# The first expert layer of a decoder on the 14 picked tokens of each batch alone

## The reference, cut to what matters

```python
B, T, C = x.shape                      # 16, 56, 128
cap = int(2.0 * T / 8)                 # 14 tokens for each of 8 experts, in each batch
probs = softmax(einsum('BTC,CE->BTE', x, gate_w), axis=-1)
top_p, top_idx = top_k(transpose(probs, (0, 2, 1)), cap)
xin = take_along_axis(x[:, None, :, :], top_idx[..., None], axis=2)
h = gelu(einsum('BElC,ECH->BElH', xin, w1), approximate=False)     # H = 512
y = einsum('BElH,EHC->BElC', h, w2) * top_p[..., None]
out = zeros((B, T, C)).at[b_idx, top_idx].add(y)
```

## Time and profile before

| | |
|---|---|
| median of 3 runs | 1523.01 us (1521.43 to 1523.82) |
| the profiled execution: its time | 1522.98 us |
| its span, first to last instruction | 1521.2 us |
| PE busy in the span | 1426.3 us (94%) |
| DVE busy | 1087.2 us (71%) |
| ACT busy | 898.9 us (59%) |
| POOL busy | 804.3 us (53%) |
| granted TensorE clock, mean | 0.973 of 2.4 GHz |

### The profile page before, as it was taken

One profiled execution on the slowest core, in us unless ns is written; L12 is line 12 of the kernel. 1 busy time (PEld: TensorE's weight loads), 2 busy tenths in 40 slices (PEclk: granted clock), 3 DMA queues, 4 the chain that ended last, 5 costly groups with the idle time before them and its releaser, 6 DMA issues.

```text
span 1521.2 us, 25506 instructions
## 1 busy us (share of the span) xinstructions
PE 1426.3 (94%) x9258; PEld 1057.2 (69%) x9258; DVE 1087.2 (71%) x2089; ACT 898.9 (59%) x1879; POOL 804.3 (53%) x440
## 2 busy tenths in 40 slices
PE   7889999999999999999999977799999999997898
PEld 4547888888888888888668644455556555553587
DVE  5538887888878888888269674677777777780587
ACT  3427666666667766666257533366666666654475
POOL 4136444444444444431046182198888888898363
PEclk9999999999999999999999998899999999997899
DMA  3032222222222222210223120454635445220221
GB/s 80 27 110 54 53 54 54 53 54 54 54 54 54 54 53 54 54 32 15 87 66 114 42 63 21 112 133 97 147 84 133 112 105 140 62 62 1 81 85 56
DMA packets 72363, 107.23 MB, mean 70 GB/s; under 512 B 14430, under 2 KB 54694, under 8 KB 72110
## 3 DMA queue, kind: packets, MB, share of 16 engines
q1 hardware_dynamic: 59326, 90.53, 24.0%
q10 hardware_dynamic: 12912, 15.08, 3.3%
HBM read 66.52 MB, written 2.08 MB: 45 GB/s over the span
## 4 chain that ended last, share of the span: by engine, by line
PE 84%; DVE 8%; issue 2%; ACT 2%; POOL 2%; DMA 1%; SPq 1%; ACTq 0%; POOLq 0%; DVEq 0%
PE PS L637 9%; PE PS L1014 7%; PE PS L651 6%; PE PS L625 5%; PE PS L1028 5%; PE PS L994 5%; PE PS L626 5%; PE PS L627 5%; PE PS L653 5%; PE PS L652 5%; PE PS L1331 4%; PE PS L1333 3%; PE PS L1332 3%; PE PS L959 3%; PE PS L965 3%
## 5 line engine op out<-in xcount | busy, mean ns | idle before, releaser
L1117 POOL TENSOR_TENSOR QO_area<-QO_area,prob_a 125x896 f32<-125x896 f32 x160 | 336.0, 2100 | 27.8 <-ACT prob_a L1202 6.4
L796 ACT ACTIVATE HL<-PS 125x512 fp32r<-125x512 f32 (+1 forms) x384 | 206.6, 539 | 178.6 <-PE PS L637 159.4
L880 DVE TENSOR_TENSOR HL<-PS,HL 125x512 fp32r<-125x512 f32 (+1 forms) x384 | 237.8, 622 | 75.9 <-ACT HL L796 56.1
L1266 DVE TENSOR_REDUCE QO_area<-PS 112x1 f32<-112x500 f32 x384 | 238.6, 670 | 66.3 <-PE PS L994 66.3
L1202 ACT ACTIVATE prob_a<-PS 125x448 f32<-125x448 f32 x384 | 187.6, 540 | 108.4 <-PE PS L1014 105.4
L710 POOL TENSOR_TENSOR HL<-ctx_area,ones 125x512 fp32r<-125x512 f32 (+1 forms) x64 | 93.1, 1454 | 247.1 <-PE PS L653 195.5
L651 PE MATMUL PS<-HL 125*128 125x512 f32 (+1 forms) x384 | 155.6, 405 | 3.6 <-DVE HL L880 3.3
L625 PE MATMUL PS<-HL 128*128 128x500 f32 x336 | 152.9, 455 | 5.6 <-POOL HL L713 5.6
L1014 PEld LDWEIGHTS PS<-HL 98*125 98x125 f32 x768 | 103.9, 188 | 72.0 <-ACT prob_a L1202 38.2
L806 ACT ACTIVATE prob_a<-prob_a,neg_max 128x500 f32<-128x500 f32 x192 | 135.5, 706 | 29.7 <-DVE neg_max L872 28.4
L994 PE MATMUL PS<-HL 96*112 96x500 f32 x384 | 129.6, 414 | 22.9 <-DVE QO_area L1266 12.3
(11 more groups left out here) (200 smaller groups left out, 2995.1 us busy)
## 6 DMA issues: line engine op xcount, KB each, us to landing
HL<-prob_b SPq DMA_DIRECT2D x128, 187.5 KB, 4.0
ctx_area<-in_ctx_T SPq DMA_DIRECT2D x16, 750.0 KB, 13.1
ctx_area<-in_ctx SPq DMA_DIRECT2D x16, 750.0 KB
HL<-ctx_area SPq DMA_DIRECT2D x64, 187.5 KB, 3.8
QO_area<-gates_kept ACTq DMA_DIRECT2D x16, 448.0 KB, 3.7
inv_area<-in_ctx_T SPq DMA_DIRECT2D x8, 750.0 KB, 4.5
prob_a<-in_ctx_T SPq DMA_DIRECT2D x8, 750.0 KB, 4.3
inv_area<-inv_kept ACTq DMA_DIRECT2D x16, 256.0 KB, 3.4
```

The costliest lines, as they stand in the source:

```text
L880: nc.vector.tensor_tensor(pL[k % 3][0:KC, 0:width(g)], PS[0:KC, 2 + k % 3, 0:width(g)], pH[k % 3][0:KC, 0:width(g)].bitcast(fp32), ALU.sub ...
L1117: nc.gpsimd.tensor_tensor(late_acc[b % 2], before, late_p[n % LATE_P], ALU.add).then_inc(m["padd"], 1)
L1266: nc.vector.tensor_reduce(late_part[b % 2][:, u // NKB, u % NKB:u % NKB + 1], PS[0:2 * S, u % NKB, 0:KB], AX, ALU.max).then_inc(m["mx"], 1)
```

## The change

The first expert layer gets functions of its own (sparse_*), and the second keeps the old ones. In the new ones every expert sees only its picked tokens, 224 columns (256 in the products, since the operands reach into what lies beside).

- **Gather.** PE turns XN into rows of tokens for each batch. DVE makes the mask of picks, PE turns it and multiplies it with a triangular matrix of ones (a running count, so each picked token gets a slot from 1 to 14), and DVE compares the slots with 1 to 14 to get a one-hot matrix of 56 x 112 (8 experts x 14 slots) for each batch. Sixteen fp32 products of token rows with one-hot matrices give the picked columns, split by ACT and DVE into xg_hl.
- **Experts.** Each has 12 matmuls for the hidden tiles and 12 for the output, of 256 columns; one gelu, one high and one low part over 4 x 224 = 896 elements, and a copy of 224 output columns. Order on PE: hidden product of expert e + 2, then output product of expert e.
- **Put back.** 16 transposes of the outputs, copies, and 16 products with `scatter` (112 x 896: the gate where the row's slot is the token's, else 0) give the sum over experts; DVE adds it to X once. `scatter` is made from the gates and the slots, which go to DRAM and come back by 16 loads of 14 partitions each, all on SP's queue.
- **Weights.** Four buffers for each weight in place of two (WBUF), and POOL starts to split when the last scores of the cross-attention are done. SP loads experts 0 and 1 before it takes back vo_kept, experts 2 and 3 after the last softmax transposes, 4 to 7 as buffers come free.
- **Constants** (a ramp of 1 to 14, the triangular matrix) are made on DVE behind the cross-attention.

The diff, cut to its core:

```diff
+            for b in range(B):
+                mm = nc.tensor.transpose(PS[0:S, b // 4, (b % 4) * 128:(b % 4 + 1) * 128],
+                                         XN[:, b * S:(b + 1) * S], ident[:, :])
...
+            hold_clock(2)
+            pe.wait_ge(m["gates"], 1)
+            nc.tensor.transpose(PS[:, 5, 0:S], routed, ident[0:S, 0:S]).then_inc(m["gtr"], 1)
+            hold_clock(3)
+            pe.wait_ge(m["picked"], 1)
+            nc.tensor.transpose(PS[0:S, 4, 64:192], work[:, 0:S], ident[:, :]).then_inc(m["slots"], 1)
+            pe.wait_ge(m["mtc"], 1)
+            nc.tensor.matmul(PS[0:S, 4, 192:320], tri[1], mask_T, start=True, stop=True).then_inc(m["slots"], 1)
+            hold_clock(1)
+            for i in range(4):
+                pe.wait_ge(m["bankc"], i + 1)
+                pe.wait_ge(m["hot"], i + 1)
+                for j in range(4):
+                    b = 4 * i + j
+                    mm = nc.tensor.matmul(PS[:, i, j * SLOTS:(j + 1) * SLOTS], tok_rows[:, b, :],
+                                          onehot[:, b, :, :].rearrange("p e r -> p (e r)"), start=True, stop=True)
+                mm.then_inc(m["bank"], 1)
...
+            def hidden_product(e):
+                pe.wait_ge(m["w1sp"], e + 1)
+                if e == 0:
+                    pe.wait_ge(m["bankc"], 8)
+                    pe.wait_ge(m["xlo"], 4)
+                if e >= 2:
+                    pe.wait_ge(m["hact"], e - 1)
+                first, off = picked_at(e)
+                for f in range(NF):
+                    mm = three_passes(PS[:, 2 * (e % 2) + f // 2, (f % 2) * 256:(f % 2 + 1) * 256],
+                                      [w[:, f * 128:(f + 1) * 128] for w in sw1_hl[e % WBUF]],
+                                      [x[:, first:first + 256] for x in xg_hl], True, True)
+                mm.then_inc(m["h"], 1)
...
+            hidden_product(0)
+            hidden_product(1)
+            for e in range(E):
+                if e + 2 < E:
+                    hidden_product(e + 2)
+                output_product(e)
...
+            pool.wait_ge(xa0["scores"], UNITS * B)
+            for e in range(E):
+                i = e % WBUF
+                pool.wait_ge(ld_sw[i], 32 * (e // WBUF + 1))
+                if e >= WBUF:
+                    pool.wait_ge(m["h"], e - WBUF + 1)
+                halve(sw1_hl[i], sw1[i], m["w1sp"])
+                if e >= WBUF:
+                    pool.wait_ge(m["y"], e - WBUF + 1)
+                halve(sw2_hl[i], sw2[i].rearrange("p g d -> p (g d)"), m["w2sp"])
...
+            sp.wait_ge(m["kept"], 32)
+            for dst, kept in ((gate_re, gates_kept[0]), (slot_re, slot_kept)):
+                for e in range(E):
+                    sp.dma_start(dst[e * CAP:(e + 1) * CAP, :],
+                                 kept[e * B:(e + 1) * B, :].rearrange("(a b) s -> a (b s)", a=1)
+                                 .broadcast_to([CAP, NTOK])).then_inc(ld_re, 16)
...
+            low(0)
+            low(1)
+            for e in range(E):
+                keep_output(e)
+                if e + 2 < E:
+                    low(e + 2)
+                if e == 2:
+                    dve.wait_ge(ld_re, 16 * 2 * E)
+                    nc.vector.scalar_tensor_tensor(scatter, slot_re, slot_col, gate_re, ALU.is_equal, ALU.mult)\
+                        .then_inc(m["scat"], 1)
...
             cross_sync(sp)
+            for e in range(2):
+                sparse_weights(sp, e)
             take_fold(sp)
...
-            experts_sync(sp, 0)
+            for e in range(2, E):
+                sparse_weights(sp, e)
+            sparse_sync(sp)
```

More of the change, by code:

```diff
@@ L263, in decoder_kernel @@
         names = "logit gexp gsub gates gtr picked kept rows xsp w1sp w2sp h hact hhi hlo y ymul b2mm".split()
-        ff = [{n: sem(f"ff{l}_{n}") for n in names} for l in range(2)]
-        ld_w = [[sem(f"ld_w{l}{i}") for i in range(2)] for l in range(2)]
-        ld_gates = [[sem(f"ld_gates{l}{i}") for i in range(2)] for l in range(2)]
+        ff = {n: sem(f"ff_{n}") for n in names}
+        ld_w = [sem(f"ld_w{i}") for i in range(2)]
+        ld_gates = [sem(f"ld_gates{i}") for i in range(2)]
+        names = "mtc hot bank bankc xlo slots slc kept wbe scat h hact hhi hlo y yc ytcd out".split()
+        sf = {n: sem(f"sf_{n}") for n in names}
+        for n in "logit gexp gsub gates gtr picked w1sp w2sp".split():
+            sf[n] = ff[n]
+        ld_sw = ld_w + [sem(f"ld_sw{i}") for i in range(2, WBUF)]
+        ld_re = sem("ld_re")
         class Chain:
@@ new lines, in sparse_gpsimd, with halve @@
+        def sparse_gpsimd(pool):
+            m = sf
+            def halve(hl, x, signal):
+                nc.gpsimd.tensor_tensor(hl[0], x, ones[:, 0:1].broadcast_to([128, FF]), ALU.mult)\
+                    .then_inc(pool_step, 1)
+                pool_count[0] = pool_count[0] + 1
+                pool.wait_ge(pool_step, pool_count[0])
+                nc.gpsimd.tensor_tensor(hl[1], x, hl[0].bitcast(fp32), ALU.subtract).then_inc(signal, 1)
+            pool.wait_ge(xa0["scores"], UNITS * B)
[8 more added lines that the diff above has]
+                halve(sw2_hl[i], sw2[i].rearrange("p g d -> p (g d)"), m["w2sp"])
@@ L1329, in experts_tensor @@
+        def experts_tensor(pe, n):
+            m = ff
+            pe.wait_ge(xn_ready, 2 * n + 2)
+            for b in range(B):
+                mm = nc.tensor.matmul(PS[0:S, 6, b * WCOLS:(b + 1) * WCOLS], XN[:, b * S:(b + 1) * S],
+                                      gate_w[1][:, :], start=True, stop=True)
             mm.then_inc(m["logit"], 1)
@@ L1488, in experts_scalar, with experts_vector @@
                         high(e + 1, f - 1)
-            if l == 0:
-                nc.scalar.preload_act_table(ACT.Sqrt)
-        def experts_vector(dve, l, chain):
-            m = ff[l]
-            ng = E if l == 0 else WCOLS
+        def experts_vector(dve, chain):
+            m = ff
             G = gate[:, :, 0:E]
@@ L1505, in experts_vector @@
             st = [gate_stat[:, k, :] for k in range(4)]
[L1506 to L1513 removed]
+            dve.wait_ge(m["logit"], 2)
@@ L1514, in experts_vector @@
+            logits = PS[0:S, 6, 0:B * WCOLS].rearrange("p (b e) -> p b e", b=B)
+            chain.link(dve, nc.vector.tensor_tensor(
+                gate[:, :, :], logits,
+                gate_b[:, :].rearrange("p (a e) -> p a e", a=1).broadcast_to([S, B, WCOLS]), ALU.add))
             chain.link(dve, nc.vector.tensor_reduce(st[0], G, AX, ALU.max))
             nc.vector.tensor_tensor(G, G, per_batch(st[0]), ALU.subtract).then_inc(m["gsub"], 1)
-            dve.wait_ge(m["gexp"], 1)
+            dve.wait_ge(m["gexp"], 2)
@@ new lines, in experts_vector @@
+            chain.link(dve, nc.vector.tensor_reduce(st[1], gate2[:, :, :], AX, ALU.add))
+            chain.link(dve, nc.vector.tensor_scalar(st[2], st[1], 0.0, None, ALU.is_equal))
+            chain.link(dve, nc.vector.tensor_tensor(st[3], st[1], st[2], ALU.add))
+            chain.link(dve, nc.vector.reciprocal(st[0], st[3]))
+            nc.vector.tensor_tensor(by_expert, gate2[:, :, :], per_batch(st[0]), ALU.mult)\
+                .then_inc(m["gates"], 1)
+            dve.wait_ge(m["gtr"], 2)
```

359 lines of the change are left out of this document (260 added, 99 removed).

## The result

| | before | after |
|---|---|---|
| median of 4 runs | 1522.22 us (1520.83 to 1523.82) | 1482.9 us (1482.68 to 1486.01) |
| the profiled execution | 1522.98 us | 1482.68 us |
| ratio | | 0.975, 95% interval 0.9733 to 0.9768 |

A forecast was written before the change was run, and what follows sets the result against it. PE bounds the old stage, POOL the new one. 15.9 + 33.9 + 5.1 = 54.9 us for 88.2, so -33.3, and -1.9 earlier: 1522.98 - 35.2 = 1487.8, about 1488 us; range 1480 to 1500, the forecast's own 1483 to 1493.

The forecast's parts named there:

- POOL takes over: Expert stretch: POOL's weight splits are slowest from expert 4 on, 4.7 to 6.9 us an expert against PE's 2.9.
- a, the front: From the first logits product to the first hidden product: 15.9 us (14.3 to 19), with the gather's clock uncertain.
- b, the experts: From the first hidden product through the expert products: 33.9 us (28.5 to 40), set by POOL's splits slowed by DVE.
- rival 1: Experts: POOL runs free of DVE and the clock stays up; stretch 28.7 us, total 1482 to 1483; chance 0.15.
- c, putting back: Stage's end, output copy, transposes, scatter products and additions to X: 5.1 us (4.5 to 7), against 2.2 before.
- d, the end of the cross-attention: 1 MB of loads out of the inv_kept write's way, so ACT should not wait: -1.9 us (0 to -2.8).
- Costed at nothing: DVE's constants behind the cross-attention's last product (about 5 us uncovered) and the scatter matrix's loads, delay up to 6 us free.
- rivals 4 and 5: Scatter loads late by 8 to 12 us, total 1490 to 1494, chance 0.07; or landing serially, about 1 us slower, chance 0.02.
- one of the three signs that the prediction named for being wrong: Wrong if PE never waits for POOL, stage clock is near 0.5, or next layer's norm starts at another clock level.
- rival 2: Whole stage: the clock stays at 1.2 GHz, a 256-column pass taking 0.213 us; total 1500; chance 0.13.
- rival 3: Experts: a 256-column pass costs what 448 columns cost, 0.20 us; stretch near 41 us, total 1495; chance 0.04.

The follow-up runs named there:

- more_bufs: Against the changed kernel: six split buffers for w1 and five for w2 instead of four each, w1 of the next expert split before w2; 1478.73 us, ratio 0.9719.
- two_pass: The changed kernel without the third pass (low x high) of the new expert products, 128 passes instead of 192; 1482.31 us, ratio 0.9746.
- no_fill: The changed kernel without the six filler products on PE between the logits and the gather; front 18.40 us, 1492.28 us in one run.
- low_memset: The changed kernel with the low part of the hidden values set to zero by DVE instead of computed; 1481.64 us, ratio 0.9741.
- late_loads: The changed kernel with the loads of experts 0 and 1 back behind the projection weights, as before the change; 1488.77 us in one run.
- before_2: The kernel before the change, unchanged, run again for a second trace; 656.3 us behind the stage, against 658.5 in the first.
- after_2: The changed kernel, unchanged, run again for a second trace; experts 33.32 us, 1484.31 us in one run.
- after_3: The changed kernel, unchanged, run again on one chip with a repeat of more_bufs; experts 33.34 us, 1484.76 us, ratio 0.9759.

## Why the prediction was right

**What bounds the kernel, and that POOL takes over** held: PE was idle between products, POOL worked without a pause from 797.06, and more_bufs and two_pass show it from both sides (less waiting for POOL: -6.5; less work for PE: -0.8 to -1.8).

**a, the front: 15.4 for 15.9.** The terms were each right within some tenths. The clock, "the question here", was full through the gather, where I took a value between full and half. The fillers did it, as no_fill shows.

**b, the experts: 32.4 for 33.9**, and three terms moved in it. Output product 0 ended 7.8 behind the first pass (7.3 predicted, with 1.1 in it for a low clock; 16 passes at 0.213 for 0.119 are 1.5, and in the other two traces of after, with about 27 such passes, it ended at 8.7). The six splits took 815.0 - 797.06 = 17.95 where I had 14.1 + 5.2 = 19.3: the loss to DVE is 17.95 - 14.1 = 3.85. Five DVE instructions with two inputs lie in that time (low parts 2 to 5 and `scatter`), so 0.77 for each, as predicted from the earlier trace rows; I had counted six and a half. In low_memset the same six splits took 2.8 us less with four of the five gone, 0.7 for each. By the Trainium skill, "SBUF — State Buffer", section "Who interferes with whom", the port lock would cost POOL the whole of each DVE instruction. The traces agree on who disturbs whom (the memsets of low_memset, with no input, cost POOL nothing). On the amount the trace of after does not: DVE's low part itself took 1.62 beside POOL for 1.09 alone, and POOL lost less than that. The one `scatter` of low_memset came nearer to it: there POOL lost 0.96 (2.00 for 1.04) and `scatter` took 1.03. Last, the 48 passes behind w1 of expert 7 took 6.6 for 5.8 + 1.5: the clock did fall in a gap that POOL left, but the slow passes were hidden. The low bound of this term was summed wrongly: 33.9 less 5.2 for contention and 1.1 and 1.5 for the clock is 26.1, not 28.5, so rival 1, with a clock that stays up, would have begun near 1480 and not at 1482.

**c, putting back: 6.7 for 5.1**, near the top of its range of 4.5 to 7. The term that was mis-sized is "the last four products (0.5)": the products fill two halves of X one after another, 16 instructions each, so all 3.74 us of L1444 stand in the path, and 1.85 lie between the two additions. From the end of the last copy (824.15 + 0.69 = 824.84) to the end of the products (827.69) it is 2.85 for the 0.5.

**d, the end of the cross-attention: -2.2 to -2.6 for -1.9.** 16.18 and 16.61 us from the vo_kept issue to the last product in two traces of before, 13.99 to 14.01 in three of after. late_loads brings the wait back with the loads alone. The last of the four loads left at 731.23, after the write's own issue at 730.90, and not just before it as the prediction has it; the other three left before.

**Costed at nothing.** The scatter loads were in time: `scatter` ran at 805.15, right behind low part 4, with no wait shown, so rivals 4 and 5 did not occur. The constants left no mark: from the last product of the cross-attention to the logits it takes 33.59 us before (740.87 to 774.46; 34.31 in before_2) and 33.59 after (740.29 to 773.88). That everything behind the stage is carried over is where the total is off: -6.0 in this pair of traces, mostly wander. And one of the three signs that the prediction named for being wrong did come: the norm behind the stage started at 0.50 of the clock over its first 2.3 us, for the 0.68 of the earlier trace rows (0.55 in after_2 and after_3, 1.00 in before_2). It is a loss, and it is not what made the stretch behind shorter.

**The rivals.** Rival 1 (POOL free of DVE) is refuted by the 2.02 of L1457, rival 2 (1.2 GHz throughout) by the windows, rival 3 (0.20 a pass) by the pass itself: 0.119 at full clock.

**How much of the number is luck.** Between the two profiled executions the stage gave 33.7 (33.3 predicted), d gave 2.2 (1.9 predicted), the 1.6 that the trace of after was late by the vo_kept issue went against it, and the stretch behind the stage gave 6.0 (0 predicted): 33.7 + 2.2 - 1.6 + 6.0 = 40.3. The two parts that the change accounts for make 35.9, so the terms fit better than the total of 39.3 lets it seem, and the 4 us between 35.2 and 39.3 are wander for the most part. Beside after_3, on one chip, the difference of the medians was 1521.32 - 1484.76 = 36.6.

## What to carry to other kernels

Where a change takes away most of the bound's work, go through the other engines with their contended rate and ask what each can have ready beforehand: here three more of POOL's buffers, with the splits in another order, gave back 6.5 to 7 us at the same speed of the splits, and faster splits (low_memset) 2 to 3. Look at where an idle gap of TensorE lies as well as at how long it is: the same gap cost nothing ahead of work that was itself covered, and 2.1 us ahead of the last products, of which fillers brought 1.3 back. And count a load's place in the queue by the small writes that go behind it.

## What was not expected of the hardware

- A product of few fp32 columns is no cheaper than a wider one. L1444 (56 columns) took 3.74 us for 32 instructions and L1433 (128 columns) 1.96 for 16: a distance of 0.11 in both, taking off the last one's length. Only the logits (8 columns, 32 in 1.82) went below, and their weights have 56 columns where those of L1444 have 128. The next row shows the weight loads in the same time, which suggests that they set it; no run took them away.

```profile
L1444 PEld LDWEIGHTS PS<-QO_area 112*128 112x128 f32 x32 | 3.7, 193 | 0.0
```

- One fp32 filler product of 448 columns is 0.75 us at full clock (two instructions, whose starts lie 0.37 to 0.38 apart; the 6.17 us of eight hold the last one's own length), as long as six 256-column passes of the fp32r kind at 0.119.
- After gaps of 3.83 and 3.90 us the passes came 0.213 apart for several us; with 3.42 ahead of it, in two_pass, PEclk was 0.52, and low_memset had 17 such passes behind a gap of only 2.06. In every trace of the changed kernel and its variants the clock is also low for 13 to 28 of the first passes of the experts; in after that began 0.7 us behind an idle 1.34, with the gather before it at full clock.
- A write of 1.5 KB needed 5.5 us to land with 1 MB of loads issued from 1.1 us ahead of it to 0.3 us behind it on another queue, and 3.1 with those loads moved.
